# Segment sum of a graph layer: one-hots stationary in four 128x32 column tiles, edges moving as raw fp32

## What is computed

```python
h = jnp.maximum(_layernorm(x, axis=-1), 0.0)                 # 6250 x 128
agg = jax.ops.segment_sum(edge_attr, dst, num_segments=6250)  # 106250 x 128 -> 6250 x 128
z = jax.nn.relu(jnp.concatenate([agg, h], axis=1) @ W1 + b1)  # 256 -> 512
out = x + (z @ W2 + b2)                                       # 512 -> 128
```

## Time and profile before

| | us |
|---|---|
| median of three runs | 326.34 |
| lowest and highest | 325.3, 327.11 |
| span of the profiled execution (first to last instruction) | 320.9 |

### The profile page before, as it was taken

One profiled execution on the slowest core, in us unless ns is written; L12 is line 12 of the kernel. 1 busy time (PEld: TensorE's weight loads), 2 busy tenths in 40 slices (PEclk: granted clock), 3 DMA queues, 4 the chain that ended last, 5 costly groups with the idle time before them and its releaser, 6 DMA issues.

```text
span 320.9 us, 10106 instructions
## 1 busy us (share of the span) xinstructions
PE 293.4 (91%) x3270; PEld 289.1 (90%) x3270; DVE 287.6 (90%) x576; ACT 127.8 (40%) x430; POOL 186.4 (58%) x212
## 2 busy tenths in 40 slices
PE   1428999999999999999999999999999999999971
PEld 1327999999999999999999999999999999999961
DVE  5998999999999999999999999999999999993310
ACT  4140234443343543444444344354344443435240
POOL 4485374664676577577567567657756756742011
PEclk9999999999999999999999999999999999999997
DMA  6973657666666776775766666677586577400000
GB/s 199 390 276 93 219 157 236 229 213 210 221 215 219 217 241 189 235 253 149 290 223 200 216 222 209 214 229 252 168 267 236 158 257 237 140 3 16 17 18 27
DMA packets 30624, 62.29 MB, mean 194 GB/s; under 512 B 2042, under 2 KB 8936, under 8 KB 30608
## 3 DMA queue, kind: packets, MB, share of 16 engines
q1 hardware_dynamic: 29202, 60.79, 58.0%
q10 hardware_dynamic: 1406, 1.30, 1.2%
HBM read 58.88 MB, written 3.20 MB: 193 GB/s over the span
## 4 chain that ended last, share of the span: by engine, by line
PE 82%; issue 8%; DVE 4%; DMA 2%; POOL 1%; DVEq 0%; SPq 0%; POOLq 0%; ACT 0%
PE bank L833 21%; PE bank L790 19%; PE bank L847 13%; PE bank L804 9%; PE bank L802 9%; PE bank L803 9%; DMA hidden<-in_dst 2%; PE bank L814 2%; DVE low L234 1%; DVE rem L231 1%; POOL outrow L371 1%; DVE onehot L585 0%; DVE relT L647 0%; DVEq L627 0%; DVE colB L661 0%
## 5 line engine op out<-in xcount | busy, mean ns | idle before, releaser
L802 PE MATMUL bank<-onehot_h,edges 128*128 128x48 bf16 (+1 forms) x535 | 95.3, 233 | 3.7 <-DVE low L234 1.9
L804 PE MATMUL bank<-onehot_h,low 128*128 128x48 bf16 (+1 forms) x535 | 96.8, 237 | 0.0
L803 PE MATMUL bank<-onehot_h,rem 128*128 128x48 bf16 (+1 forms) x535 | 96.7, 235 | 0.0
L790 PE MATMUL bank<-onehot,edges 128*128 128x48 f32 x600 | 78.3, 280 | 4.7 <-DVE base_tab L678 4.0
L234 DVE TENSOR_TENSOR low<-rem 128x640 bf16<-128x640 f32 x84 | 82.4, 981 | 0.0
L790 PEld LDWEIGHTS bank<-onehot,edges 128*128 128x128 f32 x600 | 77.1, 203 | 5.0 <-issue 4.9
L231 DVE TENSOR_TENSOR rem<-edges 128x640 f32<-128x640 f32 x84 | 79.4, 945 | 0.0
L580 DVE TENSOR_TENSOR onehot_h<-relT_h,iota_h 128x240 bf16<-128x240 bf16 x107 | 73.7, 688 | 1.3 <-DVE base_tab L678 0.9
L802 PEld LDWEIGHTS bank<-onehot_h,edges 128*128 128x128 bf16 (+1 forms) x535 | 62.8, 117 | 5.5 <-issue 4.4
L495 ACT ACTIVATE hidden<-bank,b_col 128x256 f32<-128x256 f32 (+1 forms) x100 | 41.4, 467 | 63.9 <-PE bank L833 63.9
L804 PEld LDWEIGHTS bank<-onehot_h,low 128*128 128x128 bf16 (+1 forms) x535 | 62.4, 117 | 0.0
(11 more groups left out here) (79 smaller groups left out, 489.1 us busy)
## 6 DMA issues: line engine op xcount, KB each, us to landing
edges<-in_edge_attr SPq DMA_DIRECT2D x48, 640.0 KB, 4.1
edges<-in_edge_attr SPq DMA_DIRECT2D x23, 960.0 KB, 5.1
out_rows<-outrow SPq DMA_DIRECT2D x24, 128.0 KB, 1.7
xs<-in_x SPq DMA_DIRECT2D x21, 128.0 KB, 3.7
w<-in_L_gnn_W ACTq DMA_DIRECT2D x1, 512.0 KB
xs<-in_x ACTq DMA_DIRECT2D x1, 384.0 KB, 4.5
hidden<-in_dst SPq DMA_DIRECT2D x1, 320.0 KB, 3.5
edges<-in_edge_attr SPq DMA_DIRECT2D x1, 320.0 KB
```

The lines of the kernel that those rows point to most:

```text
L790: ins = nc.tensor.matmul(sums_ps, edges[0:kp, slot, g * F:(g + 1) * F], onehot[0:kp, PLAIN.index(k), g, :], start=(g == 0), stop=(g == G - 1))
L802: nc.tensor.matmul(sums_ps, high[0:kp, cols], hot, start=(g == 0), stop=False)
L803: nc.tensor.matmul(sums_ps, middle[0:kp, cols], hot, start=False, stop=False)
L804: ins = nc.tensor.matmul(sums_ps, low[0:kp, i, cols], hot, start=False, stop=(g == G - 1))
```

## The change

The chunk becomes `G` = 3 (384 edges, 1,536 contiguous bytes a partition), and four chunks make a round of 1,536 edges, loaded by one transfer into a ring of eight. There are 69 rounds and a rest of 266 edges; block k takes the rounds that complete its 256 nodes (`ROUNDS[k]`: four, then three and sometimes two). The window is 32 nodes. No edge is split: one instruction of VectorE builds the fp32 one-hots of a whole round (384 columns). On TensorE the operands change places: the one-hot [128 edges x 32 nodes] is stationary and the fp32 edges [128 x 128 features] move. Chunk t of a round writes PSUM partitions 32t to 32t+31, so that the four chunks use four column tiles of the array. The sums come out as [nodes x features]: ScalarE copies up to four rounds from the one PSUM bank to SBUF (`copy_sums`), TensorE turns them (`turn_sums`), and VectorE adds the windows of 32 columns (`add_sums`), loading four bases for each round.

```diff
-G = 5
+G = 3
-W = 48
-SC = 7
+W = 32
+TILES = 4
+ROUND = TILES * CHUNK
+RING = 8
+HOTS = 8
...
+    ROUNDS = [list(range(rounds_by(b - 1) if b else 0, rounds_by(b))) for b in range(NB)]
...
-    high, middle = upper(edges[:, slot, :]), upper(rem[:, i, :])
-    for g in range(G):
-        hot, cols = onehot_h[0:kp, i, :, g], slice(g * F, (g + 1) * F)
-        nc.tensor.matmul(sums_ps, high[0:kp, cols], hot, start=(g == 0), stop=False)
-        nc.tensor.matmul(sums_ps, middle[0:kp, cols], hot, start=False, stop=False)
-        ins = nc.tensor.matmul(sums_ps, low[0:kp, i, cols], hot, start=False, stop=(g == G - 1))
+def sum_rounds(k):
+    if k >= 1:
+        pe.wait_ge(sums_copied, k)
+    for i, r in enumerate(ROUNDS[k]):
...
+        pe.wait_ge(edges_landed[slot], 16 * (r // RING + 1))
+        pe.wait_ge(onehot_ready, r + 1)
...
+        for g in range(G):
+            for t in range(TILES):
+                e = t * G + g
+                ins = nc.tensor.matmul(sums_ps[t * W:(t + 1) * W, cols], onehot[:, hots, e, :],
+                                       edges[:, slot, e * F:(e + 1) * F], start=(g == 0),
+                                       stop=(g == G - 1))
+def turn_sums(k):
+    pe.wait_ge(sums_copied, k + 1)
+    if k >= 1:
+        pe.wait_ge(agg_added, chunks_by(k - 1))
...
+    for i in range(len(ROUNDS[k])):
+        ins = nc.tensor.transpose(turn_ps[:, i * F:i * F + rows], sums[0:rows, k % 2, i * F:(i + 1) * F],
+                                  ident[0:rows, 0:rows])
```

VectorE's add, and its order for block k (`build` is the one-hots of a round, which may run up to eight rounds ahead):

```diff
+def add_sums(k):
+    dve.wait_ge(sums_turned, k + 1)
+    for i, r in enumerate(ROUNDS[k]):
+        cs = chunks_of(r)
+        _, bases = nc.values_load_multi_w_load_instructions(
+            base_tab[0:1, r * TILES:r * TILES + len(cs)], ...)
+        for j, c in enumerate(cs):
+            if c:
+                dve.wait_ge(agg_added, c)
+            win = aggT[:, bass.ds(bases[j], W)]
+            at = i * F + j * W
+            nc.vector.tensor_tensor(win, turn_ps[:, at:at + W], win, ALU.add).then_inc(agg_added, 1)
...
+for k in range(NB):
+    if k >= 1:
+        add_sums(k - 1)
+    rest_of_h(k)
+    if k >= 1:
+        rest_of_agg(k - 1, (k - 1) % 2, k - 1)
+    if k >= 3:
+        finish(k - 3, (k - 3) % 2, k - 3)
...
+    if k + 1 < NB:
+        for r in ROUNDS[k + 1]:
+            build(r)
+        add_b2(k + 1)
```

TensorE's and ScalarE's order for block k:

```diff
+for k in range(NB):                      # TensorE
+    sum_rounds(k)
...
+    if k >= 1:
+        layer1(k - 1, (k - 1) % 2, k - 1)
+    if k >= 2:
+        layer2(k - 2, (k - 2) % 2, k - 2)
+    turn_sums(k)
+    if k + 1 < NB:
+        turn_x(k + 1)
+for k in range(NB):                      # ScalarE
+    h_out(k)
+    if k + 2 < NB:
+        means(k + 2)
+    if k >= 1:
+        round_agg(k - 1, (k - 1) % 2, k - 1, chunks_by(k - 1))
+    if k + 2 < NB:
+        sum_squares(k + 2)
+    copy_sums(k)
+    if k + 2 < NB:
+        normalise(k + 2)
+    if k >= 1:
+        relu(k - 1, (k - 1) % 2, k - 1)
```

More of the change, by code:

```diff
@@ L28 @@
 AX_X = mybir.AxisListType.X
-G = 5
+G = 3
 CHUNK = P * G
-W = 48
-SC = 7
+W = 32
[3 more added lines that the diff above has]
+HOTS = 8
 BLOCK = 2 * P
-LEAD = 6
+SLACK = 3 * CHUNK
 WIDE = 512
[L37 to L43, removed]
+CLEARS = 8
 def graph_layer(nc, x, dst, edge_attr, W1, b1, W2, b2, out):
@@ new lines, in _ @@
+            sp.dma_start(dstD[:, :], dst[FULL * CHUNK:E].rearrange("(a e) -> a e", a=1)).then_inc(dst_landed[3], 16)
+            for r in range(1, RING):
+                load(r)
+            for k in range(NB):
+                if 3 <= k + 3 < NB - 1:
+                    load_x(k + 3)
+                if k >= 3:
+                    store(k - 3, (k - 3) % 2, k - 3)
+                for r in ROUNDS[k]:
+                    if r + RING < NROUNDS:
+                        load(r + RING)
+            for b in range(NB - 3, NB):
+                store(b, b % 2, b)
@@ L416, in _ @@
+            nc.gpsimd.tensor_copy(limit[:, :], limit_i[:, :]).then_inc(limit_ready, 1)
+            n = NWIDE * WIDE // CLEARS
+            for i in range(CLEARS):
+                nc.gpsimd.memset(aggT[:, i * n:(i + 1) * n], 0.0).then_inc(agg_cleared, 1)
+                if i < 2:
+                    spread(i)
+            for b in range(2, NB):
+                spread(b)
         @block.scalar
@@ L478, in round_agg @@
                 act.wait_ge(agg_added, added)
-                if not isinstance(n, int) or n >= 2:
+                if isinstance(n, int) and n >= 2:
                     act.wait_ge(hidden_summed, 2 * n - 2)
@@ L491, in relu @@
                         act.wait_ge(hidden_summed, 2 * n + t // 2 + 1)
-                    if t == 0 and not first:
+                    if t == 0 and not (isinstance(n, int) and n < 2):
                         act.wait_ge(out_summed, n - 1)
@@ L809, in turn_x @@
+            def turn_x(b):
+                w, par = width(b), b % 2
                 pe.wait_ge(xn_ready, b + 1)
-                if not first:
+                if b >= 1:
                     pe.wait_ge(hT_lo_ready, b)
@@ L815, in turn_x, with layer1 @@
                 ins.then_inc(h_turned, 1)
-            def layer1(n, par, b, tiles=range(HT)):
+            def layer1(n, par, b):
                 w = width(b)
                 pe.wait_ge(agg_lo_ready, n + 1)
-                for t in tiles:
-                    if t % 2 == 0:
-                        pe.wait_ge(hidden_ready, n * HT + t + 2)
+                for t in range(HT):
+                    if t % 2 == 0 and not (isinstance(n, int) and n == 0):
+                        pe.wait_ge(hidden_ready, (n - 1) * HT + t + 2)
                     o = hid_ps[t // 2][:, (t % 2) * 2 * w:(t % 2 + 1) * 2 * w]
```

912 lines of the change are left out of this document (400 added, 512 removed).

## The result

The change makes the kernel **slower: 341.97 us (median of 5 runs, 341.42 to 349.77) against 325.3 (322.56 to 327.11), a ratio of 1.052 with a 95% interval of 1.045 to 1.058**. The forecast was 285 us and faster, with a range of 258 to 330.

What follows compares the result with a forecast made beforehand. The old kernel was taken as bound by TensorE at 11.57 us a block, the new by VectorE's chain and TensorE at 10.0. Start 31, periods 230 and end 19 made 280 us, plus 5.4: 285 us, range 258 to 330.

Steps and rivals of the forecast that it cites:

- the forecast's line between two rows: Edge transfers: packet time read between 102 ns at 2,082 B and 45 ns at 950 B, giving 75 ns for 1,536 B.
- an add of 48 columns takes 0.196 us: VectorE's window adds: 0.18 us each plus 0.03 us to a waiting successor, 0.84 us for a round's four.
- the 0.33 taken: VectorE's load of four window starts per round: exposed time 0.33 us, within bounds of 0 and 0.6.
- Rival (c): VectorE's chain is longer, loads wholly exposed and signals dearer: 10.7 us a block, 302 us; chance 0.10.
- Each fp32 matmul is two records on the same tile: TensorE's rounds: only one tile's second record overlaps the next tile's first, 12 x 0.12, so 1.44 us a round.
- the lower bound of 0.72: TensorE's rounds: with four tiles quite side by side, 3 x 0.24 = 0.72 us a round.
- 1.44 us a round: TensorE's segment sum: time taken for 12 tiled fp32 matmuls, between bounds of 0.72 and 2.88 us.
- Rival (e), the clock: TensorE's clock drops from pausing each block; every layer 1 at 1.2 GHz costs 2.9 us more, 352 us; chance 0.03.
- the pause forecast: TensorE's wait for the remainder of agg before layer 1: under 1 us a block.
- 280.3 was added up: Whole span: start 31, 23 periods 230 and end 19 us, about 280 us.
- The 5.4 us added for the way from span to time: Whole kernel: the earlier profile's span of 320.9 us lay 5.4 under the median of 326.34, so 5.4 was added.
- The 0.3 us that the forecast allowed for the two switches: TensorE between tiled and full matmuls: up to 0.16 us a switch, two a block, 0.3 us.

Runs made afterwards that it cites:

- e3: The changed kernel with window starts as constants, so VectorE neither loads bases nor forms addresses; sums land a few nodes off: 257.62 us, ratio 0.790 to the kernel before.
- e4: The changed kernel with a block's window-start loads moved ahead of VectorE's wait for the turned sums: 290.96 us, ratio 0.894 to the kernel before.
- e1_filled: The changed kernel with 12 or 26 idle matmuls filling TensorE's pause ahead of layer 1, results unread: 297.98 us, ratio 0.915 to the kernel before.
- e6: The changed kernel with all four chunks of a round in the same column tile, their windows summed onto each other: 351.23 us (one run).
- e7: The changed kernel with tile and edge-slot loops exchanged, so six records of a tile follow each other: 308.21 us (one run).
- e0_after: The changed kernel run again unaltered, as reference for the experiments: 344.86 us (4 runs), profiled in its shortest.

## Why the prediction was wrong

What the change takes away, and what it hides, came as forecast. The first layer of block 0 starts at 32.7 us (31 forecast); TensorE waits for edges only at the start (4.4 us); q1's packets take 53.2% of 16 engines' span, which is 67 ns each for a mean of 1.4 KB, as the forecast's line between two rows gives (75 ns for 1.5 KB); a round's one-hots are 0.55 us (0.66 at most); ScalarE stays at 38%. The block with three rounds, from turn to turn, went like this:

| step | forecast, us | measured, us |
|---|---|---|
| turn to first add | 0.89 (0.56 and a load, 0.33) | 1.03 |
| 12 adds and two loads | 3.18 | 4.28 |
| rounding and remainder to layer 1 | 0.99 | 0.97 |
| layer 1 | 2.98 | 5.29 |
| layer 2 | 1.97 | 1.88 |
| sum | 10.0 | 13.45 |

1. **"an add of 48 columns takes 0.196 us; I take 0.18 for 32, plus 0.03 us until a successor that waits for it"** is the first step that failed. The width saved next to nothing (0.192 us). The 0.03 us from one dependent operation to the next came from a row whose operands had fixed addresses, and for those it holds: e3 measures 0.226 - 0.192. With addresses from registers it is 0.13, and e4 shows that loading early does not help. The load of the bases between rounds came out cheaper than the 0.33 taken: the gap there is 1.48 - 1.16 = 0.32 us, but 0.13 of it stands between any two adds, so 0.19 is the load's. In this block the 12 adds are 1.2 us longer than forecast, the two loads 0.3 shorter, and with the unexplained 0.17 the net is 1.1 us. Rival (c) at 302 us is what such a chain gives: e1_filled, the same chain with the clock kept, measures 298.

2. **"Each fp32 matmul is two records on the same tile ... so only the second record of one tile runs beside the first of the next"** failed in the other direction. Of its two premises the first held: in one tile a record starts 0.109 us after the last (e6). The second, that "records start in program order", did not: with the four tiles alternated four records start 7 ns apart, so the first record of the next tile starts ahead of the second of this one. A round is 0.64 us, below the lower bound of 0.72, because the bound used 0.12 us a record in one tile, and e6 shows 0.109. The Trainium skill ("TensorE: Matmul & The Clock Gate", section Part 3: Packing small matmuls) has tiles start about 4 ns apart, from which the forecast had an estimate of 0.73 us a round; the trace has 7 ns, and the runs are on its side and not on mine. The forecast saw that full overlap alone would leave the time at the chain's, and stopped there. It did not ask what the cheap rounds uncover: from the turn to layer 1 the chain takes 6.28 us (158.59 to 164.87); with 1.44 us a round some 5.0 us of TensorE's work would lie beside it and the pause would be 1.3; with 0.64 it is 2.8 and the pause 3.47.

3. **Rival (e), the clock, was given 0.03** and is what made the sign. Its price of 2.9 us a block was the upper end; measured are 1.8 (12.35 less the 10.5 of e1). It was set so low because matmuls after 1.08 us of idling kept their pace and because the pause forecast was "under 1 us". The first is what the row shows; the second did not hold, with 3.3 us a block measured. The pause had its size from points 1 and 2, and a rival that lies just behind two estimates, with one row (4.03 us idle, then half pace) that speaks for it, deserves more than the weight left over. So the step that failed here is the granted clock of 1.0 in the sum: layer 1 was put at 2.98 us and takes up to 5.49. Points 1 and 2 alone would have left the kernel faster than before, at 298 us.

The sum: the span is 339.4 us where 280.3 was added up. Block 0's first layer is 1.7 us late; from there to the last but one, 23 periods take 285.7 us for 230 (32.71 to 318.41), 55.7 more; and the end takes 21.0 for 19.3. Of these 59 us, e1's span of 295.4 gives 44 to the clock and 15 to the chain. The 5.4 us added for the way from span to time were some 3 too many, which by luck makes the miss smaller: they compared one execution's span with the median of others, and in every run on record an execution takes 1.7 to 2.0 us more than its own span. Against the kernel before, the period closes as well: 11.57 - 6.5 for the segment sum of before, + 1.8 for 2.75 rounds of 0.64 (66 rounds in 24 blocks), + 0.35 for turning the sums, + 3.3 of waiting (78.5 / 24), + 1.8 of slow clock is 12.3 us.

The 0.3 us that the forecast allowed for the two switches between full and tiled matmuls is in part there. The second transpose of x starts at 159.03 us and the first tiled record at 159.23: 0.20 us, where two transposes are 0.11 apart. In e6 the step back, from the last tiled record to layer 1, is 0.20 us as well. That is 0.09 us more a switch, some 0.2 a block. The Trainium skill ("TensorEngine Tiling (Array Packing)", section Key Properties) says that a change of mode drains the engine; the trace agrees, with these 0.09 us as its price.

## What to carry to other kernels

When work gets cheaper, ask first what it was covering: a serial chain on another engine does not shrink with it, and a pause of TensorE can be paid a second time by the large matmuls behind it, at half the clock (here 44 us of 342). Lay out by hand, for one period, which TensorE work stands between the producer and the consumer of such a chain, and put the largest stage there; here that was one move of `turn_sums` and 96 us. Idle matmuls in a pause are a cheap probe that parts the price of the clock from that of the pause, before anything is rebuilt.

## What the runs showed of the hardware

- Four column tiles of 128x32 with fp32 operands run fully side by side when alternated: four records start 7 ns apart, the next four 0.11 us later, 0.027 us a record on the mean against 0.109 in one tile.
- Across tiles TensorE does not keep the program's order of starts: in e7 six records of a tile follow each other, one tile alone starts them 0.109 us apart (e6), and yet they average 0.046, so later tiles' records started ahead of earlier ones'. Alternating is still 1.7 times faster than that.
- An add that waits for the add before starts 0.226 us after it with a constant address and 0.323 with one from a register. VectorE's sequencer takes 0.34 us to load four words (L478) and 0.046 us to form an address, and it forms it only when the add before has ended, 0.04 us after it:

```profile
L486 DVEq FUSED_REGOPS  x12: 46/46/46, 159.5 to 163.6; - x12
L486 DVE TENSOR_TENSOR aggT<-bank,aggT x12: 190/192/193, 159.6 to 163.7; 128x32 f32 x12
```

- The clock is not decided by the length of the pause alone. Of the blocks with a full layer 1, those at 79.07, 89.93 and 243.32 us ran at full pace (3.13 us) behind pauses of 1.82, 3.29 and 3.29 us, while the one at 152.34 fell to half pace 0.9 us after a pause of 1.83. What else decides it was not tried and stays open.
- A switch between full and tiled matmuls costs 0.09 us: 0.20 us from start to start where 0.11 is usual (e0_after, e6).
